# First expert layer in groups of 12, 20 and 32 tiles, with the first group's sends split over two blocks

## The chip, the core and the metric

The kernel runs on one core of a Trainium2 chip, as one program. A core has five engines that run side by side and meet only at semaphores: PE (TensorE, matrix products), DVE (VectorE), ACT (ScalarE), POOL (GpSimd) and SP (SyncE, which here only issues transfers). DMA engines move data between the device memory and the on-chip memory. POOL also issues transfers, the ones whose row addresses come from a table (indirect transfers).

The metric is the device time of one execution in microseconds (us), lower being better. The kernel before takes 1437.9 us, the median of three runs from 1436.93 to 1439.31.

## The reference, cut to what matters

The model takes an input of 8 images of 128 channels and 32 x 32 places, which is 8192 tokens of 128 numbers, or 64 tiles of 128 tokens. It runs a convolutional attention, a whitening, a linear attention, a first mixture of experts with Gelu, a window attention and a second mixture of experts with Silu. The change lies in the first mixture of experts:

```python
logits = xt @ Wr + br
probs = jax.nn.softmax(logits, axis=-1)
top_p, top_idx = jax.lax.top_k(probs, TOP_K)          # 2 of 8 experts for each token
weights = top_p / top_p.sum(axis=-1, keepdims=True)
...
h = jax.nn.gelu(jnp.einsum('end,edh->enh', xe, W1) + b1[:, None, :], approximate=False)
y = jnp.einsum('enh,ehd->end', h, W2) + b2[:, None, :]
...
out = (weights[:, :, None] * sel).sum(axis=1)
```

## The kernel before, in words

**Sorting by expert.** The kernel computes only the two experts that each token has chosen. Tokens are sorted by expert through device memory. For each tile of 128 tokens POOL issues two indirect transfers, one for the first choice and one for the second, which scatter the tile's normalised rows into a scratch tensor (`send_group`, line 1419). At most three of them are under way: each waits until the third before it has landed (`FLIGHT`). SP then loads the scratch tensor in units of 256 rows (`load` in `Units.sync`, line 1518), each unit belonging to one expert. PE turns the unit (line 1567), multiplies it up (lines 1542 to 1544) and down (line 1579). DVE adds the bias (line 1663), SP stores the result (line 1524). POOL fetches the result rows of each token again (`bring`, line 1496), and DVE adds them to the tokens with their weights (`add_result`, line 1704).

**Groups.** The 64 tiles are divided into groups with scratch tensors of their own (`Plan`, line 1013), so that units of one group can run while rows of the next are still being sent. A group of n tiles has n + 7 units, whatever the choices are. In the Gelu layer the groups have 16, 16 and 32 tiles, which makes 23, 23 and 39 units, 85 in all. SP's load of a group's first unit waits until all sends of that group have landed. A scratch tensor is chosen by its number of units; the Silu layer's plan of 32, 20 and 12 tiles has groups of 39, 27 and 19 units and uses the same tensors where the numbers agree. All scratch tensors are filled with zeros by POOL in the program's first block (line 188).

**Blocks.** The program is a chain of blocks. In a block each engine has its own list of instructions. At a block's end every engine first drains, that is, it waits until what it has been given is done, then signals; POOL collects the four other signals and releases all five. Two blocks matter here:

- The **routing block** normalises the tokens, scores them, and places the tokens of the first two groups (`place`, ending at line 1365). DVE and PE then go on with scores of the second half; DVE's last work is `adjust` (lines 1257 and 1260). POOL waits for the places and sends group 0.
- The **units' block** runs steps 0 to 88. In step s PE multiplies unit s - 2 up, turns unit s, and multiplies unit s - 4 down. DVE places the third group in pieces, one in each of the steps from the eighth on. POOL sends groups 1 and 2 and then brings the results of groups 0, 1 and 2. Results of group 0 are added from step 46 on and those of group 1 from step 60 on, four tiles every three and a half steps. SP's queue alternates a load of unit u with a store of unit u - 8; a load of unit u waits until step u - 4 is done.

After the units the same block runs a window attention, whose vector work also adds group 2.

Of the kernel before, what the change touches and what calls it, by code (L numbers as in the profile page):

```python
# [1009 lines left out]
        return [scratch[n][self.units[:g].count(n)] for g, n in enumerate(self.units)]  # L1010


GELU_PLAN = Plan([16, 16, 32], [(0, 2), (2, 3)])
SILU_PLAN = Plan([32, 20, 12], [(0, 1), (1, 3)])


# [395 lines left out]

def send_group(pool, plan, g, normed, places, sorted_rows, sent):

    for k in range(2 * plan.first_tile[g], 2 * plan.first_tile[g + 1]):
        at, r = k // 2, k % 2
        if k >= FLIGHT:
            pool.wait_ge(sent.slot(k), k // FLIGHT * 16)
        pool.indirect_dma_start(  # L1419
            out=sorted_rows[g], out_offset=bass.IndirectOffsetOnAxis(ap=places[:, at, r:r + 1], axis=0),  # L1420
            in_=normed[:, at, :], in_offset=None).then_inc(sent.slot(k), 16)
# [812 lines left out]
def gelu_and_first_half(nc, ins, ident, tokens, tables, weights, router_next, sorted_rows, sorted_results):  # L2234
    kind, plan = Expert("gelu", 512), GELU_PLAN
    W = kind.width
    group_rows, group_results = (plan.of_groups(x) for x in (sorted_rows, sorted_results))
    with ExitStack() as ctx:
        t = Tools(nc, ctx)
        gates = t.sbuf("g_gates", [P, TT, 2])  # L2240
        places = t.sbuf("g_places", [P, TT, 2], I32)
# [3 lines left out]
        normed = t.sbuf("g_normed", [P, TT, C])  # L2245
        sent = Flight(t, "gx_sent")
# [3 lines left out]
        with ExitStack() as routing:  # L2250
# [11 lines left out]
            @block.sync  # L2262
            def _(sp):
                setup.sync(sp)
                tables.sync(sp)
                sp.wait_ge(setup.loaded[2], 32)

            @block.gpsimd
            def _(pool):
                route.constants_of(pool)  # L2270
                tables.gpsimd(pool)
                pool.wait_ge(route.placed, 1)
                send_group(pool, plan, 0, normed, places, group_rows, sent)

            @block.tensor
            def _(pe):
# [76 lines left out]

        @block.gpsimd
        def _(pool):
            send_group(pool, plan, 1, normed, places, group_rows, sent)
            pool.wait_ge(route.placed, 2)
            send_group(pool, plan, 2, normed, places, group_rows, sent)
            units.bring(pool, range(plan.groups - 1))
            units.bring(pool, [plan.groups - 1])  # L2360
            silu_setup.gpsimd(pool)
# [249 lines left out]
```

## Time and profile before

| what | value |
|---|---|
| median of three runs | 1437.9 us (1436.93 to 1439.31) |
| the profiled execution | 1436.42 us, of which the span from first to last instruction is 1434.7 us |
| PE busy | 1192.1 us, 83% of the span |
| DVE busy | 919.6 us, 64% |
| POOL busy | 590.4 us, 41% |
| ACT busy | 561.0 us, 39% |
| granted TensorE clock, mean over the span | 0.873 of full speed |

The page gives each engine's busy share in 40 slices of the span, 35.9 us each. A timeline gives single instructions with their start, their length and, in brackets, how long their engine had been idle before and what ended that. An instruction whose operand is a DMA transfer (`DMA_INDIRECT`, `DMA_DIRECT2D`) is the issue of the transfer; the landing comes later.

### The profile page before, as it was taken

The numbers are of one execution on the slowest core, as the hardware profiler recorded it, in microseconds if no ns is written. First come the engines' busy times: TensorE is split into PE (matmuls) and PEld (weight loads), VectorE is DVE, ScalarE is ACT, GpSimd is POOL, SyncE is SP. The second block draws the span as 40 slices with busy tenths as digits, with TensorE's granted clock in tenths as the row PEclk, the third lists the DMA queues.
The fourth block names the chain that finished last, engine by engine and source line by source line (L and its number), as shares of the span: only waits on it lengthen the run. The fifth ranks groups of instructions, "written<-read, shape, count | busy, mean of one in ns | idle before, by whom it ended". The sixth has DMA issues, their size and how long they took to land. (4 is left out here: it accounts for less than half of the span.)

```text
span 1434.7 us, 31184 instructions
## 1 busy us (share of the span) xinstructions
PE 1192.1 (83%) x11614; PEld 1030.4 (72%) x11614; DVE 919.6 (64%) x2231; ACT 561.0 (39%) x1293; POOL 590.4 (41%) x651
## 2 busy tenths in 40 slices
PE   7999998888482999999996663858489999999960
PEld 4555557677472999999994543635489999999960
DVE  4777775578661754466642876575638777788862
ACT  3444442146360655555554531533233332332310
POOL 5000002000336767757304772067300774577675
PEclk9999999899655999999997885669559999999985
DMA  8600000000402334434324110011002333334343
GB/s 321 283 0 1 0 1 9 1 1 1 141 21 69 115 119 129 123 113 119 100 64 165 51 45 2 1 47 53 26 30 67 119 112 103 104 109 117 106 133 104
DMA packets 87095, 115.66 MB, mean 81 GB/s; under 512 B 18371, under 2 KB 71142, under 8 KB 86694
## 3 DMA queue, kind: packets, MB, share of 16 engines
q1 hardware_dynamic: 65990, 62.92, 14.0%
q0 software_dynamic: 20960, 50.76, 10.9%
q8 instruction: 97, 1.59, 0.5%
q14 instruction: 48, 0.39, 0.1%
HBM read 53.19 MB, written 60.42 MB: 79 GB/s over the span
## 5 line engine op out<-in xcount | busy, mean ns | idle before, releaser
L1419 POOL DMA_INDIRECT sorted_rows<-s_normed,s_places x128 | 135.7, 1060 | 179.3 <-DVE s_places L1365 138.7
L1496 POOL DMA_INDIRECT gx_fetch<-sorted_results,g_places x128 | 132.6, 1036 | 129.4 <-DMA sorted_results<-gx_yq 66.5
L1496 POOL DMA_INDIRECT sx_fetch<-sorted_results,s_places x128 | 137.4, 1073 | 84.7 <-issue 32.8
L1579 PE MATMUL g_bank<-weights,gx_hT 128*128 x1360 | 165.7, 275 | 0.0
L1419 POOL DMA_INDIRECT sorted_rows<-g_normed,g_places x128 | 131.6, 1028 | 67.7 <-issue 36.3
L1579 PEld LDWEIGHTS g_bank<-weights,gx_hT 128*128 128x128 f32 x1360 | 158.4, 192 | 0.5 <-issue 0.5
L1542 PE MATMUL s_bank<-sx_xT_high,sx_w_now 128*128 128x256 f32 (+1 forms) x510 | 151.8, 298 | 1.1 <-DVE sx_hT L1654 0.6
L1544 PE MATMUL s_bank<-sx_xT_high,sx_w_now 128*128 128x256 f32 (+1 forms) x510 | 144.1, 283 | 0.0
L1543 PE MATMUL s_bank<-sx_xT_low,sx_w_now 128*128 128x256 f32 (+1 forms) x510 | 143.9, 282 | 0.0
L1607 ACT ACTIVATE gx_hT<-g_bank,gx_b_now 128x256 f32<-128x256 f32 x340 | 133.0, 482 | 3.0 <-PE g_bank L1579 3.0
L1579 PE MATMUL s_bank<-weights,sx_hT 128*128 (+1 forms) x1020 | 129.7, 276 | 2.9 <-DVE sx_yq L1665 1.4
L1579 PEld LDWEIGHTS s_bank<-weights,sx_hT 128*128 128x128 f32 (+1 forms) x1020 | 120.4, 191 | 6.4 <-issue 6.0
L1600 ACT ACTIVATE sx_xT_high<-s_bank 128x256 fp32r<-128x256 f32 x85 | 32.7, 385 | 225.5 <-PE s_bank L1579 207.6
L237 PE MATMUL attended<-probs,vs 128*128 128x512 f32 x256 | 120.3, 593 | 0.0
L339 ACT ACTIVATE probs<-score,nmax 128x1024 f32<-128x1024 f32 x64 | 71.4, 1115 | 113.0 <-DVE nmax L281 113.0
L281 DVE TENSOR_REDUCE nmax<-score 128x1 f32<-128x1024 f32 x64 | 78.2, 1224 | 45.5 <-PE score L226 45.5
L1542 PE MATMUL g_bank<-gx_xT_high,gx_w_now 128*128 128x256 f32 x340 | 103.7, 305 | 3.5 <-DVE gx_w_now L1637 2.1
L1663 DVE TENSOR_TENSOR gx_yq<-g_bank,weights 128x256 f32<-128x256 f32 x85 | 36.1, 425 | 100.0 <-PE g_bank L1579 97.5
L1544 PE MATMUL g_bank<-gx_xT_high,gx_w_now 128*128 128x256 f32 x340 | 96.7, 284 | 0.0
L1543 PE MATMUL g_bank<-gx_xT_low,gx_w_now 128*128 128x256 f32 x340 | 96.7, 284 | 0.0
L1600 ACT ACTIVATE gx_xT_high<-g_bank 128x256 fp32r<-128x256 f32 x85 | 32.7, 385 | 162.2 <-PE g_bank L1579 127.1
L1542 PEld LDWEIGHTS s_bank<-sx_xT_high,sx_w_now 128*128 128x128 f32 (+1 forms) x510 | 91.2, 179 | 1.7 <-issue 1.7
(423 smaller groups left out, 2729.5 us busy)
## 6 DMA issues: line engine op xcount, KB each, us to landing
sorted_rows<-zeros POOLq DMA_DIRECT2D x29, 512.0 KB, 15.5
gx_xq<-sorted_rows SPq DMA_DIRECT2D x85, 128.0 KB, 2.0
sorted_results<-gx_yq SPq DMA_DIRECT2D x85, 128.0 KB, 1.9
sx_xq<-sorted_rows SPq DMA_DIRECT2D x85, 128.0 KB, 2.1
sorted_results<-sx_yq SPq DMA_DIRECT2D x85, 128.0 KB, 2.0
feats<-in_x SPq DMA_DIRECT2D x8, 512.0 KB, 7.0
out<-tokens SPq DMA_DIRECT2D x16, 256.0 KB, 4.0
s_raw<-in_silu_up SPq DMA_DIRECT2D x1, 2736.0 KB, 9.9
```

The lines of the kernel that those rows point to most:

```text
L237: done = pe.matmul(out[:, HALF * h:HALF * h + HALF], vs[s % 4][:, :], probs[s % 4][:, HALF * h:HALF * h + HALF], start=(n == 0), stop=(n = ...
L281: dve.tensor_reduce(nmax[s % 4][:, :], score[s % 2][:, :], AX.X, ALU.max, negate=True).then_inc(max_ready, 1)
L339: act.activation(probs[s % 4][:, :], score[s % 2][:, :], ACT.Exp, bias=nmax[s % 4][:, 0:1], accum_out=zsum[s % 4][:, 0:1]).then_inc(exp_do ...
L1419: pool.indirect_dma_start(out=sorted_rows[g], out_offset=bass.IndirectOffsetOnAxis(ap=places[:, at, r:r + 1], axis=0), in_=normed[:, at, : ...
L1496: pool.indirect_dma_start(out=fetch[n % 2][:, i, r, :], out_offset=None, in_=self.sorted_results[g], in_offset=bass.IndirectOffsetOnAxis(a ...
L1542: pe.matmul(out, left[:, part, columns], right[0][:, :], start=True, stop=False)
L1543: pe.matmul(out, left[:, part, columns], right[1][:, :], start=False, stop=False)
L1544: pe.matmul(out, left[:, part + 1, columns], right[0][:, :], start=False, stop=True)
L1579: done = pe.matmul(down[u % 2][:, P * k:P * k + C], hT[u % 2][0:width, i, P * k:P * k + P], self.w_down[0:width, bass.ds(e, 1), i, :].rear ...
L1600: act.activation(xT[u % 2][0][:, :], self.turned[u % 2][:, 0:UNIT], ACT.Copy).then_inc(self.x_high, 1)
L1607: done = act.activation(hT[i][:, k, :], up[i][k // 2][:, k % 2, :], ACT.Gelu, bias=self.b_now[u % 4][:, k:k + 1])
L1663: dve.tensor_tensor(self.yq[u % 4][:, :, :], product, bias, ALU.add).then_inc(self.y_ready, 1)
```

## The change

The Gelu plan becomes 12, 20 and 32 tiles, so that the groups have 19, 27 and 39 units, again 85. The sends of the first group are divided: the first eight tiles (16 transfers) are sent in the routing block, the other four (8 transfers) are the first work of POOL in the units' block. The Silu plan stays.

```diff
-GELU_PLAN = Plan([16, 16, 32], [(0, 2), (2, 3)])
+SENT_EARLY = 8
+GELU_PLAN = Plan([12, 20, 32], [(0, 2), (2, 3)])
 SILU_PLAN = Plan([32, 20, 12], [(0, 1), (1, 3)])
...
 def send_group(pool, plan, g, normed, places, sorted_rows, sent):
 
-    for k in range(2 * plan.first_tile[g], 2 * plan.first_tile[g + 1]):
+    send_tiles(pool, g, plan.first_tile[g], plan.first_tile[g + 1], normed, places, sorted_rows, sent)
+
+
+def send_tiles(pool, g, first, end, normed, places, sorted_rows, sent):
+
+    for k in range(2 * first, 2 * end):
         at, r = k // 2, k % 2
         if k >= FLIGHT:
             pool.wait_ge(sent.slot(k), k // FLIGHT * 16)
...
                 pool.wait_ge(route.placed, 1)
-                send_group(pool, plan, 0, normed, places, group_rows, sent)
+                send_tiles(pool, 0, 0, SENT_EARLY, normed, places, group_rows, sent)
...
         @block.gpsimd
         def _(pool):
+            send_tiles(pool, 0, SENT_EARLY, plan.first_tile[1], normed, places, group_rows, sent)
             send_group(pool, plan, 1, normed, places, group_rows, sent)
             pool.wait_ge(route.placed, 2)
```

The next two pieces are POOL's list from the last work of the routing block to the end of the Gelu units. The two branches are the end of the routing block and the start of the units' block; `sorted_rows` is the scratch tensor, and its first size is its number of rows. Before:

```order
L1903 AFFINE_SELECT w_last_bias<-w_last_bias 32x16
L1419 DMA sorted_rows_0<-g_normed,g_places 5888x128 x32
L2250 UNCONDITIONAL_BRANCH
L2354 UNCONDITIONAL_BRANCH
L1419 DMA sorted_rows_1<-g_normed,g_places 5888x128 x32
L1419 DMA sorted_rows_0<-g_normed,g_places 9984x128 x64
L1496 DMA gx_fetch<-sorted_results_0,g_places 128x128 x32
L1496 DMA gx_fetch<-sorted_results_1,g_places 128x128 x32
L1496 DMA gx_fetch<-sorted_results_0,g_places 128x128 x64
```

Now (the lines of the changed file lie six or seven further down):

```order
L1909 AFFINE_SELECT w_last_bias<-w_last_bias 32x16
L1425 DMA sorted_rows_0<-g_normed,g_places 4864x128 x16
L2256 UNCONDITIONAL_BRANCH
L2360 UNCONDITIONAL_BRANCH
L1425 DMA sorted_rows_0<-g_normed,g_places 4864x128 x8
L1425 DMA sorted_rows_0<-g_normed,g_places 6912x128 x40
L1425 DMA sorted_rows_0<-g_normed,g_places 9984x128 x64
L1502 DMA gx_fetch<-sorted_results_0,g_places 128x128 x128
```

Sixteen sends have moved from before the block's end to behind it; of the 24 sends that the first unit needs, 16 stand before the block's end and 8 behind it.

SP's queue where the second group's first unit is loaded. The three counters that tell that sends have landed bear the names of earlier semaphores with the same numbers: `qk_high`, `proj_ready` and `x_loaded7`. Before, at unit 23:

```order
L1518 DMA gx_xq2<-sorted_rows23_0 128x256 [waits gx_stepped]
L1524 DMA sorted_results23_0<-gx_yq2 128x256 [waits gx_y_ready]
L1518 DMA gx_xq3<-sorted_rows23_1 128x256 [waits qk_high,gx_stepped,proj_ready,x_loaded7]
L1524 DMA sorted_results23_0<-gx_yq3 128x256 [waits gx_y_ready]
L1518 DMA gx_xq0<-sorted_rows23_1 128x256 [waits gx_stepped]
```

Now, at unit 19:

```order
L1524 DMA gx_xq2<-sorted_rows19_0 128x256 [waits gx_stepped]
L1530 DMA sorted_results19_0<-gx_yq2 128x256 [waits gx_y_ready]
L1524 DMA gx_xq3<-sorted_rows27_0 128x256 [waits qk_high,gx_stepped,proj_ready,x_loaded7]
L1530 DMA sorted_results19_0<-gx_yq3 128x256 [waits gx_y_ready]
L1524 DMA gx_xq0<-sorted_rows27_0 128x256 [waits gx_stepped]
```

The load that waits for the second group's sends stands four units earlier in the queue, with a store of results behind it.

POOL's filling of the scratch tensors with zeros in the program's first block, before and now as one difference:

```order
-L188 DMA sorted_rows_0<-zeros 128x1024 x5
-L188 DMA sorted_rows_0<-zeros 128x768
-L188 DMA sorted_rows_1<-zeros 128x1024 x5
-L188 DMA sorted_rows_1<-zeros 128x768
-L188 DMA sorted_rows_0<-zeros 128x1024 x9
+L188 DMA sorted_rows_0<-zeros 128x1024 x4
 L188 DMA sorted_rows_0<-zeros 128x768
 L188 DMA sorted_rows_0<-zeros 128x1024 x6
 L188 DMA sorted_rows_0<-zeros 128x768
-L188 DMA sorted_rows_0<-zeros 128x1024 x4
+L188 DMA sorted_rows_0<-zeros 128x1024 x9
 L188 DMA sorted_rows_0<-zeros 128x768
```

The two tensors of 23 units are gone, since 19 and 27 units are sizes that the Silu layer has too: 22 fills in place of 34.

## Rows read from the trace of the kernel before

**Rows 1.** The page: busy tenths and granted clock in 40 slices.
```profile
PE   7999998888482999999996663858489999999960
PEclk9999999899655999999997885669559999999985
```

**Rows 2.** Waits of PE, 440 to 820: us in total, times, longest.
```profile
PE g_bank L1567 <- DMA gx_xq<-sorted_rows: 23.1, 1, 23.1
```

**Rows 3.** Timeline of POOL: sends 1, 16 and 32 (start, length, operation, idle before).
```profile
414.88 1.12 POOL L1419 DMA_INDIRECT sorted_rows<-g_normed,g_places  x1 [20.80 <-DVE g_places L1365]
...
434.24 0.96 POOL L1419 DMA_INDIRECT sorted_rows<-g_normed,g_places  x1 [0.30 <-issue]
...
454.58 0.96 POOL L1419 DMA_INDIRECT sorted_rows<-g_normed,g_places  x1 [0.30 <-issue]
```

**Rows 4.** Timeline of all engines, 434 to 464: the change of blocks.
```profile
433.76 3.77 PE L1195 MATMUL gr_bank<-g_router,gr_uT 128*128 128x8 f32 x17
...
438.30 0.42 DVE L1260 TENSOR_TENSOR g_room<-g_room,g_rbias 128x256 f32<-128x256 f32 x1
...
458.55 3.67 SPq L1518 DMA_DIRECT2D gx_xq<-sorted_rows  x6
459.12 0.96 POOL L1419 DMA_INDIRECT sorted_rows<-g_normed,g_places  x1 [3.57 <-POOLq L2250]
...
460.68 1.12 PE L1567 MATMUL g_bank<-ident,gx_xq 128*128 128x128 f32 x4 [23.14 <-DMA gx_xq<-sorted_rows]
...
463.90 0.55 PE L1542 MATMUL g_bank<-gx_xT_high,gx_w_now 128*128 128x256 f32 x1 [2.10 <-DVE gx_w_now L1637]
```

**Rows 5.** Timeline, 1056 to 1064: the change of blocks before the Silu units.
```profile
1057.55 0.23 DVE L1242 COPY sr_logits<-sr_bank 128x64 f32<-128x64 f32 x1 [3.19 <-PE sr_bank L1195]
1058.12 4.79 SPq L1518 DMA_DIRECT2D sx_xq<-sorted_rows  x6
```

**Rows 6.** Timeline, 870 to 892: the change of blocks behind the first window attention.
```profile
887.79 0.69 DVE L2189 TENSOR_TENSOR tokens<-tokens,g_bank 128x512 f32<-128x512 f32 x1 [2.47 <-PE g_bank L2022]
...
889.00 0.14 POOL L1165 IOTA sr_rank_i<- 128x8 int32 x1 [21.53 <-SPq L2453]
```

**Rows 7.** DMA issues, 438.9 to 456: count, median us from issue to landing.
```profile
sorted_rows<-g_normed,g_places POOLq DMA_INDIRECT x14, 2.2
```

**Rows 8.** Windows of 1 us, 20 us: length, busy (count) by engine, PEclk, DMA, GB/s.
```profile
468.00:469.00 1.00, 1.00 (x10) 1.00 (x9) 0.28 (x2) 0.99 (x2) 0.70 (x2) 0.88 0.55 188
...
500.00:520.00 20.00, 20.00 (x177) 20.00 (x176) 13.49 (x40) 10.45 (x30) 12.76 (x14) 1.00 0.37 122
...
720.00:740.00 20.00, 20.00 (x177) 20.00 (x177) 8.90 (x23) 10.45 (x30) 0.00 (x0) 1.00 0.26 80
```

**Rows 9.** Windows of 5 us behind the Gelu units and at the Silu units' start.
```profile
795.00:800.00 5.00, 0.00 (x0) 0.00 (x0) 4.48 (x22) 1.86 (x5) 3.78 (x5) 0.59 0.19 52
...
825.00:830.00 5.00, 4.91 (x221) 3.03 (x220) 4.67 (x11) 3.53 (x7) 3.90 (x4) 1.00 0.22 59
...
1065.00:1070.00 5.00, 5.00 (x29) 5.00 (x29) 2.47 (x5) 2.20 (x4) 0.00 (x0) 0.60 0.10 30
```

**Rows 10.** POOL's groups: busy, mean ns, idle; 439 to 456, 459 to 503, 506 to 593.5.
```profile
L1419 POOL DMA_INDIRECT sorted_rows<-g_normed,g_places x14 | 13.5, 968 | 4.3 <-issue 4.3
...
L1419 POOL DMA_INDIRECT sorted_rows<-g_normed,g_places x32 | 33.1, 1036 | 14.0 <-issue 8.5 <-POOLq L2250 3.6 <-DMA sorted_rows<-g_normed,g_places 1.9
...
L1419 POOL DMA_INDIRECT sorted_rows<-g_normed,g_places x64 | 67.2, 1050 | 23.5 <-issue 18.3 <-DVE g_places L1365 3.6 <-DMA sorted_rows<-g_normed,g_places 1.3
```

**Rows 11.** Timelines: SP's load of unit 19, PE's turn of unit 19.
```profile
513.11 0.32 SPq L1518 DMA_DIRECT2D gx_xq<-sorted_rows  x1
...
524.65 0.38 PE L1567 MATMUL g_bank<-ident,gx_xq 128*128 128x128 f32 x2
```

**Rows 12.** Timelines: POOL's eighth fetch, DVE's first adds.
```profile
603.38 1.19 POOL L1496 DMA_INDIRECT gx_fetch<-sorted_results,g_places  x1 [0.30 <-issue]
...
621.53 1.38 DVE L1704 SCALAR_TENSOR_TENSOR tokens<-gx_fetch,g_gates,tokens 128x128 f32<-128x128 f32 x4
```

**Rows 13.** Windows of 15 us during the fills with zeros and behind them.
```profile
30.00:45.00 15.00, 15.00 (x57) 9.34 (x56) 9.98 (x18) 6.45 (x11) 4.72 (x9) 1.00 1.02 412
...
105.00:120.00 15.00, 15.00 (x56) 9.00 (x55) 11.38 (x22) 6.51 (x11) 0.00 (x0) 1.00 0.00 1
```

## The prediction, made before the changed kernel ran

> **What bounds the kernel now.** I read the page's slices first, for where PE is idle. Besides the very end, the emptiest is the one from 430 to 466 us (2 tenths, at a clock of 5 tenths). It lies just before the Gelu units; the eight after it are full [rows 1]. Of PE's waits between 440 and 820 us one entry matters here: 23.1 us, once, before the first turn of a unit, for the load of sorted rows [rows 2]. The timelines say how these come about. POOL's 32 sends of group 0 run from 414.88 to 455.54, one after the other [rows 3]. The other engines of the routing block are done long before: PE at 433.76 + 3.77 = 437.53, DVE at 438.30 + 0.42 = 438.72 [rows 4]. So POOL alone holds the block for 455.54 - 438.72 = 16.8 us. SP's first load follows at 458.55, the first turn at 460.68 [rows 4]. From there PE is busy without a gap: all windows of 20 us from 500 to 740 show 20.00 us at full clock, the first and the last of twelve being shown [rows 8]. What PE starts earlier, it therefore ends earlier.
>
> **The change part by part.**
>
> *The first group's sends.* Now 16 sends stand in the routing block. The sixteenth ends at 434.24 + 0.96 = 435.20 [rows 3], so the block's last engine is DVE, at 438.72.
>
> *The change of blocks.* This is the unknown of the sum. Before, 3.01 us pass from the end of POOL's last send to SP's first load, and 3.57 us to POOL's own next send [rows 4]. Elsewhere, where DVE is last and POOL has long finished its transfers, it is 1058.12 - 1057.78 = 0.34 us to SP's first load [rows 5] and 889.00 - 888.48 = 0.52 us to POOL's next instruction [rows 6]. I read the 2.7 us between 3.01 and 0.34 as POOL's drain behind a send that it has only just handed over. In the changed kernel this drain runs from 435.20 to about 437.9, beside DVE's last work; it ends 0.8 us before DVE does. Thus release to SP's queue is at 438.72 + 0.34 = 439.06, and POOL's next send, which before came 459.12 - 458.55 = 0.57 us behind SP's first load, is at 439.63. The other end is that a change of blocks costs POOL 3.57 us from the last engine's end, whoever is last; then it is 438.72 + 3.57 = 442.29. I take the first value, because two changes of blocks of this trace stand beside it.
>
> The rows do not say whether the 2.7 us belong to the drain or to POOL's way into the next code. The Trainium skill, PSUM — Partial Sum Buffer, section Engine vs sequencer instructions, says that a drain waits for the engine to go fully idle. By that rule the first value holds and the time is 1431.0 us; by a fixed cost of POOL's way the second holds and it is 1433.7 us.
>
> *The eight sends behind it.* In quiet, between 439 and 456 us, 14 sends take 13.5 + 4.3 = 17.8 us, 1.27 us each [rows 10]; PE and DVE are idle there now as before. The eighth starts at 439.63 + 7 x 1.27 = 448.52 and ends at 449.5. Landing takes 2.2 us from the issue [rows 7]. Counted from the instruction's start that is 450.7, from its end 451.7; before, it was at most the 3.01 us from the end (SP's load waits for it too), which gives 452.5. I take 451.7, between the two. This is a wait that the change of blocks used to hide and that now lies on the path.
>
> *The first load and turn.* From load to turn 460.68 - 458.55 = 2.13 us [rows 4]: the turn is at 451.7 + 2.13 = 453.8. Before it was at 460.68, so the units start **6.9 us earlier**, with bounds of 6.1 (landing at 452.5) and 7.9 (at 450.7), and of 4.2 with the dearer change of blocks (turn at 456.5).
>
> *The clock.* PE starts the units at half clock before and after, since it is idle for 16 us now and 23 us before. Full clock was granted during the window 468 to 469 [rows 8], some 9.6 us behind the first load; at the Silu units it came at about 1069, by the mean of 0.60 over 1065 to 1070 [rows 9], some 10.9 us behind the first load at 1058.12 [rows 5]. The 1.3 us between these at half clock is worth 0.65 us; I take nothing and widen the range by 1 us.
>
> *Group 1's sends* become 40 and are behind POOL's 8. Beside the units a send takes (33.1 + 14.0 - 3.6) / 32 = 1.36 us, and the 64 of group 2 (67.2 + 23.5 - 3.6) / 64 = 1.36 us too [rows 10]. From 449.8, 40 x 1.36 = 54.4 us end at 504.2, landed at about 506.4. SP's load of unit 19 was issued at 513.11 and turned at 524.65 [rows 11]; 6.9 us earlier that is 506.2 and 517.7. So the load comes 0.2 us late or not at all, and has 517.7 - 2.1 - 506.4 = 9.2 us before PE misses it. The store of unit 11 is queued behind this load; its result buffer is wanted four steps later, which is as far away. Cost nothing, cover 9.2 us.
>
> *Group 2's sends* started at 506.24, when DVE had placed them; now POOL comes to them at 504.2, and DVE's places come 6.9 us earlier and wait. Their 64 x 1.36 = 87 us end at 591. Their first load is that of unit 46 in both kernels, 27 steps behind that of unit 19. A step has 30 products (12 up, 2 turns, 16 down), and 177 in 20 us [rows 8] make it 3.4 us; so the load is wanted at about 506.2 + 27 x 3.4 = 598. The sends have landed by 593.5: covered by some 4 us, and by 9 more before PE would stop. The first eight fetches follow until about 602, landed by 605; before, the eighth was at 603.38, the first add at 621.53 [rows 12], now about 614.6. Covered by 9 us. Adds of group 1 now run four steps longer, still before the units' end.
>
> *The zero fills* are 12 fewer. While they ran, PE issued 57 products in 15 us, and 56 in an equal stretch without them [rows 13]. PE does not feel them: nothing, either way.
>
> **Sum.** The profiled execution took 1436.42 us (span 1434.7 us); less 6.9 it is 1429.5. The median of the runs lies 1.5 us above that execution, so 1437.9 - 6.9 = **1431.0 us**.
>
> **The rivals.**
>
> *A: the change of blocks costs 3.57 us whoever is last.* For: it is the only change of blocks into sends that this trace has. Against: 0.34 and 0.52 us elsewhere [rows 5, 6]. Gain 4.2 us: 1433.7 us.
>
> *B: the gain is given back later.* Behind the units the clock goes up and down (0.59 in one window of 5 us, 1.00 in another [rows 9]), and PE, DVE and POOL wait for each other there. If two more windows of 5 us fell to half clock with PE busy, 2 x 2.5 = 5 us would come back: 1437.9 - 6.9 + 5 = 1436.0 us. For: the clock there is not steady. Against: nothing in that stage is tied to a fixed time, so all of it should move with the units, and the three runs lie within 2.4 us.
>
> *C: the sends starve beside the units.* Now 40 sends, not 32, have to land for group 1, and four units sooner. The point from which it decides: 40 sends must not take more than 54.4 + 9.2 = 63.6 us to be hidden, and not more than 63.6 + 6.9 = 70.5 us, 1.76 us each, for the kernel not to be slower than before. At 1.9 us each they land at 449.8 + 76 + 2.2 = 528.0; with 2.1 us for the load unit 19 is turned at 530.1 in place of 524.65 [rows 11], and the time is 1437.9 + 5.4 = 1443.3 us. For: sends took 1.36 us beside the units and 1.27 in quiet. Against: that is a fifth of the way from 1.27 to 1.76, and it held over 96 sends [rows 10]. The Trainium skill, SBUF — State Buffer, section SBUF: two separate sides, has a rule against this change: while certain copies of VectorE run, GpSimd cannot write the descriptors of the transfers it issues. Rows 10 show at most 0.09 us of it per send.
>
> *D: the block does not end so much earlier*, because SP or ACT holds it. For: their ends are not in the rows above. Against: SP has only loads of weights there and ACT nothing that PE, done at 437.53, does not follow. If one of them held the block for 6.9 us beyond DVE, the gain would be gone: 1437.9 us.
>
> **How the numbers follow.** Forecast 0.72 (1431.0 us, 1429 to 1433 by its bounds, the clock and the scatter of the runs); A 0.14; B 0.07; C 0.03; D 0.04. A difference of 0.2%, 2.9 us, is about what measurements of this kernel can tell from none; below 1435.0 counts as faster. That is the forecast, A and a little of B: 0.87. Same: the rest of B and D, 0.09. Slower: C and a bit of the others, 0.04. The range reaches from 1428.5 (gain 7.9 and a better clock) to 1435.0 (A with 1.3 us of scatter).
>
> **What would show it.** The changed profile should have POOL's sixteenth send end near 435.2, its seventeenth start near 439.6 (442.3 by A), the 24th near 448.5, SP's first load near 451.7, and the first turn near 453.8. PE's wait before the first turn should fall from 23.1 to about 16 us. PE should be busy without a gap behind it, through unit 19 too; a wait of SP or PE there speaks for C. The end of the units should be as much earlier as their start; if it is and the span is not, B is right. A seventeenth send later than 443, or a landing more than 3 us behind the last send, would make the sum wrong.

## The result and the profile after

The changed kernel takes **1422.6 us**, the median of five runs (1419.86 to 1423.69). The kernel before, timed beside it, takes 1436.93 us (five runs, 1432.76 to 1439.31; three of them are those of the 1437.9 us). The ratio on record is 0.992, with a 95% interval from 0.9897 to 0.9944; that of the two medians is 0.990. The forecast of 1431.0 us had the right sign, but the time lies 5.9 us below the lower end of its range.

The steps around the change of blocks came nearly as forecast. The timeline of all engines in the changed kernel, from POOL's first send to the first turn of a unit (start, length, engine, line, operation, idle time before):

```profile
415.76 1.12 POOL L1425 DMA_INDIRECT sorted_rows<-g_normed,g_places  x1 [19.36 <-DVE g_places L1366]
...
435.89 0.96 POOL L1425 DMA_INDIRECT sorted_rows<-g_normed,g_places  x1 [0.30 <-issue]
439.17 0.42 DVE L1261 TENSOR_TENSOR g_room<-g_room,g_rbias 128x256 f32<-128x256 f32 x1
440.73 0.96 POOL L1425 DMA_INDIRECT sorted_rows<-g_normed,g_places  x1 [3.89 <-POOLq L2256]
449.58 0.96 POOL L1425 DMA_INDIRECT sorted_rows<-g_normed,g_places  x1 [0.31 <-issue]
451.88 11.51 SPq L1524 DMA_DIRECT2D gx_xq<-sorted_rows  x8
453.99 1.20 PE L1573 MATMUL g_bank<-ident,gx_xq 128*128 128x128 f32 x4 [15.58 <-DMA gx_xq<-sorted_rows]
```

The rows are the first, sixteenth, seventeenth and 24th send, DVE's last work of the routing block, SP's first load and PE's first turn. This execution began its sends 0.88 us later than the one of [rows 3]; so distances from the first send compare better than clock times. First send to first turn is 453.99 - 415.76 = 38.23 us; it was 460.68 - 414.88 = 45.80 [rows 3, 4]. That is **7.6 us less**.

PE's wait before the first turn, in the waits of PE from 440 to 820 us:

```profile
PE g_bank L1573 <- DMA gx_xq<-sorted_rows: 15.6, 1, 15.6
```

It was 23.1 us [rows 2]. From 500 us on PE has no gap. Two windows of 20 us (columns as in [rows 8]), then SP's load and PE's turn of unit 19, then POOL's 64th send, which is the last one that this load needs:

```profile
500.00:520.00 20.00, 20.00 (x178) 20.00 (x176) 11.20 (x32) 10.70 (x30) 14.99 (x15) 1.00 0.38 126
...
720.00:740.00 20.00, 20.00 (x178) 20.00 (x176) 9.18 (x24) 10.65 (x29) 0.00 (x0) 1.00 0.22 67
```

```profile
506.58 0.32 SPq L1524 DMA_DIRECT2D gx_xq<-sorted_rows  x1
...
518.07 0.38 PE L1573 MATMUL g_bank<-ident,gx_xq 128*128 128x128 f32 x2
```

```profile
504.01 1.16 POOL L1425 DMA_INDIRECT sorted_rows<-g_normed,g_places  x1 [0.30 <-DMA sorted_rows<-g_normed,g_places]
```

Both rows of unit 19 stand 6.5 to 6.6 us earlier than in [rows 11]. That is the first turn's 6.7 us but for 0.1 to 0.2: the 40 sends of group 1 landed in time.

So 6.7 us of this execution's gain stand at the units' start. But the two profiled spans differ by 1434.7 - 1421.4 = 13.3 us. The rest is not where the change is. It shows in the page's slices (40 of 35.5 us):

```profile
PE   7999998888574999999996673858589999999960
...
PEclk9999999899655999999997885779569999999985
```

Compared with [rows 1], the dip around the thirteenth slice is shallower, as the shorter wait before the first turn makes it. The granted clock has 7 and 7 in the 26th and 27th slice where it had 6 and 6, and 6 in the 30th where it had 5: that is the stretch of the second window attention. The same stretch by windows, from the Silu routing's first statistics (`sr_norm_bn`) to the first Silu turn; columns as in [rows 8], so the second number is the length and the third PE's busy time. Before:

```profile
894.07:1060.11 166.04, 116.42 (x2394) 90.21 (x2394) 92.69 (x271) 64.95 (x137) 62.84 (x64) 0.67 0.09 29
```

After:

```profile
886.05:1047.46 161.41, 111.08 (x2395) 88.53 (x2395) 92.70 (x271) 64.87 (x137) 62.32 (x64) 0.69 0.10 30
```

The same products take PE 5.3 us less at a higher granted clock, and the stretch is 4.6 us shorter; DVE, ACT and POOL are as busy as before. The other 2 us lie before and behind this stretch, 1.4 and 0.7 us (the rows "before" and "changed" of the table below). Had the change done this, or had the two executions only happened to differ? The experiments ask that first.

### The profile page after: what moved, and what is told of

Same layout as the page of the kernel before. It is cut to its first block and busy times, and to the rows that moved or that the text cites. A ratio compares the mean times of both kernels' runs of the same rounds, so it can differ in the third digit from the quotient of the medians.

```text
span 1421.4 us, 31172 instructions
## 1 busy us (share of the span) xinstructions
PE 1188.9 (84%) x11614; PEld 1028.8 (72%) x11614; DVE 919.4 (65%) x2231; ACT 560.4 (39%) x1293; POOL 582.9 (41%) x639
## 5 line engine op out<-in xcount | busy, mean ns | idle before, releaser
L1425 POOL DMA_INDIRECT sorted_rows<-g_normed,g_places x128 | 132.4, 1035 | 64.8 <-issue 35.4
```

The source lines that it names most:

```text
L1425: pool.indirect_dma_start(out=sorted_rows[g], out_offset=bass.IndirectOffsetOnAxis(ap=places[:, at, r:r + 1], axis=0), in_=normed[:, at, : ...
```

## The experiments

Two theories. **Scatter:** the change gives what it gives between the first send and the first turn, and the rest is the clock in the window attentions, which differs from one execution to the next of any kernel. **A second effect:** something else in the change (the shared scratch tensors, the twelve fills that are gone, the new phase of later work) makes the later stretches shorter.

For every traced execution five stretches can be read from the timelines: *start* (POOL's first send to the first Gelu turn), *units* (to PE's last product of the units), *window 1* (to `sr_norm_bn`), *window 2* (to the first Silu turn) and *end*. The experiments come below; the table stands first because all of them lean on it. "Start + units" is what remains when the clock's scatter is set aside, against the 345.5 us of before (mean of two). The time ahead of the first send, 413.6 to 416.4 us in these traces, is left out; its spread follows no kernel.

| kernel | start | units | window 1 | window 2 | end | start + units against before | ratio of times (95%) |
|---|---|---|---|---|---|---|---|
| before | 45.80 | 299.8 | 133.6 | 166.0 | 374.6 | | |
| before again (e5) | 45.59 | 299.8 | 132.4 | 166.3 | 374.9 | | 0.9998 (0.9979 to 1.0016) |
| changed | 38.23 | 299.9 | 132.2 | 161.4 | 373.9 | -7.4 | 0.992 (0.9897 to 0.9944) |
| changed again (e1) | 38.26 | 300.1 | 132.9 | 163.0 | 373.8 | -7.1 | 0.9942 (0.9918 to 0.9965) |
| changed again (e11) | 38.27 | 300.1 | 132.0 | 160.4 | 373.9 | -7.1 | 0.9944 (0.9922 to 0.9965) |
| e2, 24 sends early | 35.70 | 299.9 | 133.1 | 165.5 | 373.7 | -9.9 | 0.9933 (0.9907 to 0.9959) |
| e2 again (e10) | 35.68 | 299.9 | 131.5 | 161.2 | 374.7 | -9.9 | 0.9937 (0.9916 to 0.9958) |
| e9, 18 early | 37.02 | 299.9 | 133.4 | 160.1 | 373.6 | -8.6 | 0.9924 (0.9905 to 0.9943) |
| e3, own scratch | 38.18 | 300.1 | 133.4 | 165.7 | 373.8 | -7.2 | 0.9936 (0.9912 to 0.996) |
| e4, 12 early | 43.32 | 300.0 | 134.3 | 160.8 | 374.8 | -2.1 | 0.9994 (0.9976 to 1.0012) |
| e6, split alone | 48.32 | 299.8 | 132.5 | 161.3 | 374.9 | +2.7 | 1.0014 (0.9997 to 1.003) |
| e7, POOL late | 46.81 | 299.8 | 131.5 | 163.1 | 374.7 | +1.1 | one run |
| e8, first group of 8 | 26.39 | 317.9 | 133.1 | 160.3 | 373.9 | -1.2 | 0.9991 (0.9976 to 1.0005) |

### The changed kernel again (e1, e11) and the kernel before again (e5)

No edit. They ask what executions of one and the same kernel differ by.

> The changed kernel again, beside the kernel before. Theory 1 (start plus clock): the change gives the 6.7 us that the two traces show at the first turn (460.68 against 453.99), and the other 6.6 us of the profiled difference are a clock in the two window attentions that differs from execution to execution; then the medians lie 6 to 9 us apart and single times of the two kernels scatter by 4 us or more. Theory 2 (a second gain): something else in the change, the fills or the shared scratch tensors, gives another 5 us in every execution; then the medians lie 11 to 14 us apart and every stage behind the units is shorter in every trace of the changed kernel. Theory 3 (phase): the window attentions run faster or slower by when they start; then 11 to 14 us too, and it is the later starts that tell.

> The kernel before, measured against itself, to see what its own executions differ by. If the base was the prediction's mistake, the time lies near 1432 us and not at 1437.9, with single runs from 1427 to 1438, the ratio is 1.000 within 0.25%, the stretch from POOL's first send to the first turn is 45.8 us within 0.3 as in the trace that the prediction used, and the stretch from the second window attention to the first Silu turn differs from that trace's 166.0 us by some us, shorter with a higher granted clock there. If the median of 1437.9 was the kernel's own time and the lower times of later calls belong to a better chip, the changed kernel and this one move alike and nothing in that stretch need differ: 166 us again.

> The changed kernel a third time, for comparison on the same chip: 38.2 us from the first send to the first turn, 300 us of units, and 6 to 10 us less than the kernel before. If the stretch from the second window attention to the first Silu turn scatters from execution to execution, it may lie anywhere from 160 to 167 us.

Measured: changed 1423.76 us (seven runs, 1421.93 to 1426.58), and on another chip 1423.18 (eight runs, 1420.01 to 1429.37). The kernel before against itself: 1433.09 us (twelve runs, 1424.92 to 1436.02) beside 1430.79 (29 runs, 1427.05 to 1437.95). The experiments ran on three chips (e1 to e4, e5 to e8, e9 to e11), and the kernel before, timed on each beside them, has medians of 1431.75, 1430.79 and 1433.03 us over 19, 29 and 13 runs. With the twelve of e5 these are 73 later runs of it. On the second chip alone they reach from 1424.92 to 1437.95 us, so single runs of one kernel on one chip lie up to 13 us apart, and no later series has a median near 1437.9. The start stretch repeats within 0.2 us.

The mean granted clock of each run is on record. In the 73 runs it reaches from 0.868 to 0.882; the 16 runs at 0.873 or less have a median of 1434.6 us, the 12 runs at 0.880 or more one of 1428.9 us. So the times of one and the same kernel go with the clock that was granted. In which stretch a run was granted less, only a trace tells.

That one and the same kernel differs in the second window is not shown by the two traces of before, which have 166.0 and 166.3 us (e5 expected a shorter one if the base was the mistake, and missed there), but by other kernels traced more than once: 160.4, 161.4 and 163.0 for the changed one, and, clearest, the pair of e2, below.

### The scratch tensors of before (e3)

```diff
-        return [scratch[n][self.units[:g].count(n)] for g, n in enumerate(self.units)]
+        return [scratch[n][-1 if self is SILU_PLAN else 0] for n in self.units]
...
-        scratch.setdefault(units, max(plan.units.count(units) for plan in (GELU_PLAN, SILU_PLAN)))
+        scratch.setdefault(units, 1 if units == 39 else 2)
```

Gelu and Silu have scratch tensors of their own again, and as much is filled with zeros as before.

> The changed kernel with scratch tensors of 19 and 27 units of their own for the Gelu and the Silu layer, so that 131 units of zeros are filled as in the kernel before, in place of 85. Theories 1 and 3: no difference to the changed kernel (within 1.5 us). Theory 2: it loses about 5 us and lies 6 to 7 us below the kernel before.

Measured: 1423.76 us, the changed kernel's time on the same chip (e1), and the same start and units. Its one trace has a second window of 165.7 us, as long as before's, but the median of its seven runs is the changed kernel's all the same. Shared tensors and fewer fills are worth nothing that can be measured. The second effect has lost its likeliest carrier.

### All 24 sends in the routing block (e2, e10)

```diff
-SENT_EARLY = 8
+SENT_EARLY = 12
```

> Groups of 12, 20 and 32 tiles, all 24 sends of the first group in the routing block. POOL's 24th send then ends at 436.85 + 8 x 1.27 = 447.0, SP's first load follows 3.0 us later as before (drain and release), at 450.0, and the first turn at 452.1, 1.9 us earlier than in the changed kernel, since the landing of the last send is hidden under the drain. Theories 1 and 2: 1.9 us faster than the changed kernel. Theory 3: the time may move by several us either way, while the first turn moves by 1.9.

> All 24 sends of the first group in the routing block, measured again beside the changed kernel on one chip. From the first send to the first turn 35.7 us within 0.2, 2.5 us less than the changed kernel's 38.2. The time is expected 2.5 us lower, which the scatter of some 3 us in the interval may hide; if it comes out level or higher again, something behind the units takes it back, and the stretch from the second window attention to the Silu units, 165.5 us in its first trace, should again be longer than the 161.4 and 163.0 us of the changed kernel's traces.

Measured: 1424.04 us (six runs, 1418.91 to 1426.32) and 1423.15 (six runs, 1420.6 to 1428.01), beside 1423.76 and 1423.18 for the changed kernel. The timeline of e2 has the last send, SP's first load, POOL's next send and the first turn:

```profile
445.39 0.95 POOL L1425 DMA_INDIRECT sorted_rows<-g_normed,g_places  x1 [0.30 <-issue]
448.95 3.64 SPq L1524 DMA_DIRECT2D gx_xq<-sorted_rows  x6
449.52 0.95 POOL L1425 DMA_INDIRECT sorted_rows<-g_normed,g_places  x1 [3.18 <-POOLq L2256]
451.06 1.16 PE L1573 MATMUL g_bank<-ident,gx_xq 128*128 128x128 f32 x4 [13.04 <-DMA gx_xq<-sorted_rows]
```

The start is 2.6 us shorter than in the changed kernel, in both traces (e2 expected 1.9). The eight sends behind the change of blocks are thus no help: the smaller group alone brings 10.0 us, and the split takes 2.6 of them back. In the changed kernel POOL stands idle for 3.89 us between its sixteenth and seventeenth send, so its 24th starts 3.8 us later behind the first one than here (33.82 for 30.03 us); the load follows that send's start by 2.30 us in place of 3.56, which gives 1.3 back. In the times those 2.6 us don't show: the twelve runs of e2 and e10 are on average 0.5 us below the fifteen of e1 and e11, with some 2 us either way, so 2.6 us lies at the edge of what they leave open. What else moves, the two traces of this same kernel show. The second window of e2:

```profile
884.02:1049.48 165.46, 116.50 (x2394) 90.33 (x2395) 92.62 (x271) 65.20 (x137) 62.33 (x64) 0.67 0.09 29
```

The second window of e10, the same code on another chip:

```profile
883.05:1044.21 161.16, 111.24 (x2395) 88.60 (x2395) 92.80 (x271) 64.92 (x137) 62.35 (x64) 0.70 0.10 30
```

It is 4.3 us shorter, with PE busy 5.3 us less at a higher granted clock, and with all else alike: the same pair of rows as before against after. So this difference needs no change of the kernel. But it does not tell where the 2.6 us went: e10 expected a long second window should the time come out level with the changed kernel's, and it came out level with a short one.

Over all 13 traces of the table the four second windows of 165 us and more have a mean granted clock of 0.66 to 0.67, the nine shorter ones of 0.69 to 0.71. That both traces of before are among the four could still be more than chance, as only two of the other eleven are. The times speak against it: in the nine later comparisons with the kernel before (e1 to e4, e6, e8 to e11) the difference of the mean times departs from the column start + units by -2.4 to +1.9 us, on average by -0.3 us. A second effect of 5 us has no room there, so **Scatter** holds. What makes the clock differ is not settled: the three traces of the third chip (e9 to e11) all have 160 to 161 us, while those of each of the first two reach from 160 to 166.

### The split without the smaller group (e6)

```diff
-GELU_PLAN = Plan([12, 20, 32], [(0, 2), (2, 3)])
+GELU_PLAN = Plan([16, 16, 32], [(0, 2), (2, 3)])
```

> Groups of 16, 16 and 32 tiles again, and 16 of the first group's 32 sends behind the change of blocks. If the prediction's arithmetic holds, each send behind the change costs 1.265 us: from the first send to the first turn 38.2 + 8 x 1.265 = 48.3 us, which is 2.5 us more than before (45.8), so the kernel is 2.5 us slower than before: some 1434 us beside 1431.75, ratio 1.0017. If the gain comes from splitting the sends and not from the smaller group (the block ending earlier lets something else start earlier), it is faster than before by some us.

Measured: a start of 48.32 us against the 48.3 worked out, and 1432.49 us, a ratio of 1.0014 (0.9997 to 1.003). Each of the eight further sends behind the change of blocks costs (48.32 - 38.25) / 8 = 1.26 us of the start, where 1.265 was expected. Splitting alone loses.

### Twelve sends early (e4), eighteen early (e9)

```diff
-SENT_EARLY = 8
+SENT_EARLY = 6
```

and 9 in place of 8 for e9.

> The changed kernel with 6 tiles sent in the routing block and 6 behind it. Four more sends then lie behind the change of blocks: the first turn is at 453.99 + 4 x 1.27 = 459.1, only 1.6 us earlier than before. Theory 1: 5.1 us slower than the changed kernel, about 1.6 us below the kernel before. Theory 2: 5.1 us slower than the changed kernel, but 6 to 7 us below the kernel before. Theory 3: the time does not follow the start; it may lie several us off 5.1.

> Groups of 12, 20 and 32 tiles with nine of the first group's tiles (18 sends) in the routing block, six sends behind it. The 18th send ends about 23.3 us behind the first one's start, 0.5 us before DVE's last work. If a send just handed over holds POOL for some 1.2 us or more beyond its end, next to what the change takes anyway, POOL signals last: its next send comes 25.6 to 26.5 us behind the first, and the first turn 36.5 to 37.2 us. If the dearer change is paid only where POOL's last instruction ends last, the next send comes 24.97 us behind the first as with eight tiles, and the first turn 35.7 us, as early as with all 24 sends in the routing block. In time that is 1.0 to 2.5 us less than the changed kernel, below what one call resolves.

Measured for e4: a start of 43.32 us, 5.1 longer than the changed kernel's, as expected, and 1432.14 us. The interval of its ratio contains the 0.9985 that 2.1 us make, and not the 0.995 to 0.996 that 6 to 7 us by a second effect would make. For e9: 1422.06 us (six runs, 1419.98 to 1424.19), ratio 0.9924. Its timeline has the eighteenth send, DVE's last work, the nineteenth send, the first load and turn; its first send is at 414.90:

```profile
437.29 0.95 POOL L1425 DMA_INDIRECT sorted_rows<-g_normed,g_places  x1 [0.30 <-issue]
438.31 0.42 DVE L1261 TENSOR_TENSOR g_room<-g_room,g_rbias 128x256 f32<-128x256 f32 x1
441.17 0.95 POOL L1425 DMA_INDIRECT sorted_rows<-g_normed,g_places  x1 [2.93 <-POOLq L2256]
449.82 3.66 SPq L1524 DMA_DIRECT2D gx_xq<-sorted_rows  x6
451.92 1.21 PE L1573 MATMUL g_bank<-ident,gx_xq 128*128 128x128 f32 x4 [14.37 <-DMA gx_xq<-sorted_rows]
```

DVE ends last here, at 438.73, half a us behind POOL's send at 438.24, and yet POOL's next send is not 1.14 us behind DVE as in the changed kernel but 2.44 us. It is 2.93 us behind POOL's own last send: POOL's way through the change, not DVE's, sets it. With sixteen sends early that way lay hidden beside DVE; with eighteen it takes half of the 2.5 us that more early sends could gain (38.2 to 35.7 us): the start is 37.02. That is the first of the two expectations.

### POOL last without a fresh transfer (e7)

```diff
                 send_tiles(pool, 0, 0, SENT_EARLY, normed, places, group_rows, sent)
+                steps = Steps(pool, blank_steps)
+                for _ in range(10):
+                    steps.then(pool.memset(blank[:, :], 0.0))
```

> The changed kernel with ten fillings of an unused tile (about 0.95 us each) as POOL's last work of the routing block, behind its 16 sends, so that POOL is the last engine of the block, at about 445 to 446 us, with its last transfer handed over 10 us earlier. If the 2.7 us at the change of blocks are POOL's drain behind a fresh transfer, its next send comes 0.5 to 1.2 us behind the last filling, and from the first send to the first turn it is about 45 us. If they belong to POOL's way into the next block whenever POOL is last, the next send comes 3.2 to 3.6 us behind it, and that stretch is about 47.5 us.

Measured, POOL's fillings and its next send:

```profile
437.45 10.04 POOL L2283 MEMSET gr_blank<- 128x1024 f32 x10
...
449.92 0.96 POOL L1425 DMA_INDIRECT sorted_rows<-g_normed,g_places  x1 [2.44 <-POOLq L2256]
```

2.44 us lie between the end of the last filling, 447.49, and the next send. Both theories miss: one said 0.5 to 1.2, the other 3.2 to 3.6. This is one trace, and ends of POOL's instructions are rough in a profile. With POOL last and its transfers 10 us old it is 2.44; with POOL last and a fresh send 3.17 to 3.57 (e10, e2, before); behind DVE with POOL long done 1.14. So of the extra cost of ending a block with sends, 1.3 us come with POOL being last at all, and 0.7 to 1.1 us with the fresh transfer. Why POOL's being last costs 1.3 us stays open. POOL also has to collect the four other signals, and when it is last it may come to all of that late; no run tests this.

### A first group of eight tiles (e8)

```diff
-GELU_PLAN = Plan([12, 20, 32], [(0, 2), (2, 3)])
+GELU_PLAN = Plan([8, 24, 32], [(0, 2), (2, 3)])
```

This is rival C's mechanism brought about on purpose: 48 sends have to land before unit 15.

> Groups of 8, 24 and 32 tiles, the first all in the routing block. The first turn then needs no send behind the change: DVE ends about 23.8 us behind POOL's first send, the load follows at 0.6 and the turn 2.1 us later, 26.5 us in all in place of 38.2. But 48 sends x 1.36 us = 65 us must land before unit 15, from about 440.7 to 508 with landing, turn at about 510; without a wait unit 15 would be turned at 442.3 + 15 x 3.37 = 493. If sends beside the units hold to 1.36 us, PE waits 17 us once before unit 15, the stretch of the units grows from 300.4 to about 318 us (more if the clock falls in the wait), and the kernel is 6 us slower than the changed one, 1429 to 1433 us. If sends that are waited for go at the quiet pace of 1.27 us, the wait is 13 us and it is 2 us slower.

Measured: 1431.1 us, ratio 0.9991 to before; the start is 26.39 us (26.5 expected), the units take 317.9 (318 expected). PE's turns of units 13, 14 and 15:

```profile
485.58 0.38 PE L1573 MATMUL g_bank<-ident,gx_xq 128*128 128x128 f32 x2
489.01 0.38 PE L1573 MATMUL g_bank<-ident,gx_xq 128*128 128x128 f32 x2
507.47 0.69 PE L1573 MATMUL g_bank<-ident,gx_xq 128*128 128x128 f32 x2 [14.86 <-DMA gx_xq<-sorted_rows]
```

DVE's last work of the routing block, SP's first load, and POOL's first and last of the 48 sends:

```profile
439.37 0.42 DVE L1261 TENSOR_TENSOR g_room<-g_room,g_rbias 128x256 f32<-128x256 f32 x1
440.36 15.86 SPq L1524 DMA_DIRECT2D gx_xq<-sorted_rows  x9
440.93 0.95 POOL L1425 DMA_INDIRECT sorted_rows<-g_normed,g_places  x1 [3.95 <-POOLq L2256]
...
503.15 0.96 POOL L1425 DMA_INDIRECT sorted_rows<-g_normed,g_places  x1 [0.30 <-DMA sorted_rows<-g_normed,g_places]
```

From 440.93 to 504.11 they take 1.32 us each, between the quiet price and the price beside units. PE waits 14.9 us, about 2 less than the 17 expected, and then turns at 1.8 times the length (0.69 for 0.38 us): the granted clock is 0.50 from 505 to 510 us, half of full speed (1.2 of 2.4 GHz), and 1.00 again from 515 us. The units grow by 18 us all the same. So the 318 came out right partly by luck: the wait was shorter than expected, and the lower clock behind it made up for that. What the earlier start gave, 11.8 us against the changed kernel, the wait takes back and 6 us more. So a first group can be too small. With 12 tiles the second group's sends land just before their load is issued: the 64th started at 504.01, and 2.3 us later is 506.3, for a load at 506.58. Sizes between 8 and 12 tiles were not run.

## Why the prediction was wrong

**Right: what bounds the kernel, and the mechanism.** POOL's sends held the block, the units moved as a whole, and the wait before the first turn fell to 15.6 us (about 16 forecast). Rival A is out: the seventeenth send came 440.73 - 439.59 = 1.14 us behind DVE's end, where A asked for 3.57. Rival C did not come about with 40 sends, and e8 shows it with 48. D is out by the same rows as A. B took nothing that shows: the column start + units gives a ratio inside the measured interval in every row but that of the first comparison, where 7.4 us make 0.9948 and the interval ends at 0.9944.

**Right in size, with two small misses that cancel in part.** The change of blocks was put at 0.34 + 0.57 = 0.91 us; it took 1.14. In e8, where SP's load waits for no send behind the change, that load came 440.36 - 439.79 = 0.57 us behind DVE, not 0.34 as at the Silu units, and POOL's send another 0.57 us behind it. The landing was put at 2.2 us from the end of the 24th send; SP's load came at 451.88, 1.34 us behind its end and 2.3 behind its start. So the 2.2 us of [rows 7] fit a count from the instruction's start, the bound that I had and did not take. Together the first turn came 0.7 us sooner behind the first send than forecast, 38.23 for 453.8 - 414.88 = 38.92.

**Right by a reason that was only half right.** I read the 2.7 us of [rows 4, 5] as a drain behind a fresh send, and forecast that it would be hidden beside DVE with 0.8 us to spare. It was hidden, and e9, with the cover taken away, shows it come out: in these traces POOL's next send comes 1.14 us behind DVE or some 2.4 to 3.6 us behind POOL's own last instruction, whichever is later. The prediction left open whether the 2.7 us belong to the drain or to POOL's way into the next code. In before, e2, e10 and e8 alike POOL's next send follows SP's first load by 0.57 us, while that load comes 3.01, 2.61 and 2.60 us behind the end of a block that POOL ends with a send and 0.57 us behind one that DVE ends (e8). So the surplus lies ahead of the release, not on POOL's way behind it. But e7 shows that the fresh send is the smaller part of it. The Trainium skill, PSUM — Partial Sum Buffer, section Engine vs sequencer instructions, says that a drain waits until the engine is fully idle. The surplus of 0.7 to 1.1 us with a fresh send agrees with that; the other 1.3 us it does not explain, since the fillings had ended by the profile.

**Wrong: the base, in the step Sum, and the scatter, in the step How the numbers follow.** I subtracted 6.9 us from 1437.9, the median of three runs, and let the runs scatter by about a us, because the three lay within 2.4 us. In the 73 later runs of the kernel before on three chips, all from 1424.92 to 1438.13, the medians are 1430.8 to 1433.1 us, and only three runs reach 1436.9. From 1431.75 the same 6.9 us give 1424.9, and the changed kernel measured 1422.6, 1423.8 and 1423.2. Of the miss of 8.4 us some 6 are the base and 0.7 the two terms above; the last us or two are within the scatter of the runs, and no run shows more about them. The gain itself reads 14.3 us beside the high first runs of before, and 8.0 (e1) and 9.9 us (e11) by the later medians, where the start stretch and the units give 7.1 to 7.4. Rival B saw the unsteady clock behind the units, but I priced it as a consequence of the change and in one direction alone. It belonged into the base, both ways.

That three of three runs lay where only three of 73 do is hardly chance within one population. The two further runs of before in the first comparison read 1432.76 and 1434.3. The traced execution of 1436.42 us had a mean clock of 0.873, as the slower of the later runs have; the clock of the first three runs is not on record, and what set them apart stays open.

## What to carry to other kernels

Take the difference that a change makes from the stretch in which it acts, and measure it there: the start stretch repeated within 0.2 us while whole runs lay up to 13 us apart. Three runs that agree do not bound the scatter of a kernel with stretches of short bursts at a changing clock; look in such a stretch for what one execution more could give or take, and put it into the base of a forecast, in both directions.

When sends feed a pipeline in groups, a smaller first group helps as long as the second group's sends still land in time (12 tiles here, but not 8); what is moved behind a change of blocks pays its full price per send. Of the variants here, all 24 sends in the routing block has the shortest start and units together, 2.6 us less than the changed kernel, but none is faster than the changed kernel by more than these times can tell.

## What the runs showed of the hardware that was not expected

- The granted clock in the second window attention differs between executions of one and the same code: 0.67 and 0.70 on average in two traces of e2's kernel, with PE busy 116.5 and 111.2 us for the same products, and the stretch 165.5 and 161.2 us long.
- A change of blocks costs POOL 1.14 us to its next send when DVE is last and POOL long done (0.57 us to SP's load and 0.57 us more to the send, in e8), 2.44 us when POOL is last with fillings, and 3.17 to 3.57 us when it is last with a fresh indirect transfer. With a send that ends half a us ahead of DVE it is 2.93 us behind that send (e9).
- The load that waited for the 24th send came 2.30 us behind the start of the instruction that issues it and 1.34 us behind its end; in e7 and e9 it was 2.32 and 2.33 us behind the start. All these sends last 0.95 to 0.96 us, so the traces do not tell which of the two ends counts.
